# Last layer of a decoder kernel: expert outputs scattered with an add into four DRAM accumulators, in place of eight rows a token

## The chip, the cores and the metric

The kernel runs on one core of one Trainium2 chip. The metric is the time of one execution on the device in microseconds (us); smaller is better. The core has five engines with a queue of instructions each: TensorE (PE; PEld are its weight loads), VectorE (DVE), ScalarE (ACT), GpSimd (POOL) and SyncE (SP). Sixteen DMA engines move data between DRAM and the on-chip memories. Engines wait for one another and for transfers by semaphores.

## The reference

The program is a stack of four layers, each a cross attention and a feed-forward stage with a residual, on x of 8 x 128 tokens of 256 values. Only the last stage, a mixture of 64 experts of which each token takes 8, and each expert at most 128 tokens, bears on the change:

```python
x_rep = jnp.repeat(x, K, axis=0)                                  # K = 8
xe = jnp.zeros((E, C, H), x.dtype).at[flat_e, pos].set(x_rep, mode='drop')   # E = 64, C = 128
gu = jnp.einsum('ech,ehf->ecf', xe, gate_up_proj)
g, u = jnp.split(gu, 2, axis=-1)
h = jax.nn.silu(g) * u
ye = jnp.einsum('eci,eih->ech', h, down_proj)
valid = pos < C
y_flat = jnp.where(valid[:, None], ye[flat_e, jnp.minimum(pos, C - 1)], 0.0)
y = jnp.sum(y_flat.reshape(-1, K, H) * topw.reshape(-1, K)[..., None], axis=1)
...
x = x + _L3_ffn_ref(_layernorm(x, axis=-1), ...)
```

So a token's result is the sum of up to eight expert rows, each times its weight, and x.

## The kernel before

The whole program is written by hand, engine by engine; each stage is a block in which every engine has its own list of instructions in a fixed order, and blocks end in a barrier. Nothing plans the order: what stands in the code is what each queue holds. The last stage is the function `moe_l3`. It has four parts.

**Routing** (PE, DVE, ACT). PE makes the router's logits. DVE finds each token's eight experts (L2334 to L2340, `mask`). From the mask two things are made side by side: PE counts each token's place in its expert's list (`pos`, L2241, 36 small matmuls), and DVE makes a key for every token and expert. The key holds the number of the DRAM row into which this expert's result for this token will go: 8 x token + rank, and the rank comes from a running count over the mask (L2344, L2345, L2347). L2349 then needs both. After a transpose, eight rounds of maximum and replace (L2358, L2361) list each expert's 128 largest keys, and L2364 to L2367 turn these into `slot` (the row for the scatter) and `idx` (the token, slot divided by eight, for the gather). Slots that hold no token point at rows behind the tokens' rows.

**The expert loop.** For each of 64 experts POOL issues an indirect DMA that gathers 128 token rows of x (L2208), PE transposes them and multiplies by the gate and up weights (L2269), ACT and DVE make h, PE transposes h (L2277) and multiplies by the down weights (L2284), ACT scales the rows by the routing weights into one of four buffers `ye` (L2326), and POOL issues an indirect DMA that scatters the 128 rows of 1 KB to DRAM (`rows`, L2213). POOL issues eight gathers first and then, for each scatter, two gathers until 16 are ahead, then one; the last 16 scatters have no gathers between them. Before ACT overwrites a buffer of `ye` it waits until the scatter of four experts ago has landed:

```python
                    if e >= NY:
                        act.wait_ge(put[e % NY], 16 * (e // NY))
```

SP meanwhile loads the experts' weights, 16 loads of 1280 KB, six loads ahead of their use (L2183).

**The sum.** When all scatters have landed, SP reads the rows back in eight loads of 1024 KB, one for each 128 tokens (L2187; each token's eight rows are 8 KB in one piece). DVE adds eight rows to four, to two, to one (L2397) and adds x (L2398), and SP stores the 128 tokens (L2190).

**Zeroing.** A token whose expert was full has no row, so `rows` is set to zero beforehand: eight writes of 1024 KB that SP issues in the attention of layer 1 (L837), some 1100 us earlier. POOL waits for them before the first scatter.

Of the kernel before, what the change touches and what calls it, by code (L numbers as in the profile page):

```python
# [9 lines left out]
I32 = mybir.dt.int32  # L10
U8 = mybir.dt.uint8
U32 = mybir.dt.uint32
ALU = mybir.AluOpType
# [3 lines left out]
P = 128  # L17
D = 256
KD = D // P
B = 8  # L20
T = B * P
# [763 lines left out]
def attention_l1(pg):  # L785
# [5 lines left out]
    const, masks, qm_in, cb_in, vz_in, scores, maxed, nm_turned, augmented, shifted, exped, pv, recip, scaled, added = (  # L791
        pg.sem(f"l1x_{m}") for m in sems)
    with ExitStack() as st:
# [39 lines left out]

        @block.sync
        def _(sp):
            for i in range(8):
                sp.dma_start(pg.l3_rows[T * i:T * (i + 1), :].rearrange("(p r) d -> p r d", p=P),  # L837
                             pg.zero_row[:].unsqueeze(1).to_broadcast([P, T // P, D])).then_inc(pg.rows_zeroed, 16)

# [1278 lines left out]
def moe_l3(pg, pre, xw, rows):  # L2118

    nc, E, K, CAP, F = pg.nc, 64, 8, 128, 96  # L2120
    GROUP, LOADS, AHEAD, FIRST, NY = 4, 6, 16, 8, 4
# [6 lines left out]
    s = {m: pg.sem(f"l3m_{m}") for m in names}  # L2128
    w_in = [pg.sem(f"l3m_w_in{i}") for i in range(LOADS)]
    gathered = [pg.sem(f"l3m_gathered{i}") for i in range(AHEAD)]  # L2130
    put = [pg.sem(f"l3m_put{i}") for i in range(NY)]
    back = [pg.sem(f"l3m_back{i}") for i in range(B)]
    with ExitStack() as st:
        def sb(m, shape, dt=F32):
            return st.enter_context(nc.sbuf_tensor(f"l3m_{m}", shape, dt))
        def wide_of(at, n):
            return pg.l2_wx[:].rearrange("p k n -> p (k n)")[:, at:at + n].rearrange("p (b e) -> p b e", b=B)
# [2 lines left out]
        cw = wide_of(512, B * E)  # L2140
        left = wide_of(1024, B * E)
        mask = sb("mask", [P, B, E], BF16)
        tmp = wide_of(2048, B * E)
        best = sb("best", [P, B, 8])
        top = sb("top", [P, B, 8])
        small = sb("small", [P, 3, B])
# [2 lines left out]
        token = sb("token", [P, B])  # L2149
        row = sb("row", [P, E])  # L2150
        key = wide_of(2560, 2 * B * E)
        spent = pg.l2_w3[:].rearrange("p a k n -> p (a k n)").bitcast(F32)
# [1 line left out]
        lst = sb("lst", [P, CAP // 2])  # L2154
        spare = sb("spare", [P, E])
        idxf = sb("idxf", [P, E])
        count = pg.l2_wx[:].rearrange("p k n -> p (k n)")[:, 3584:3584 + B * E]
        slot = sb("slot", [P, E], I32)
        idx = sb("idx", [P, E], I32)
        zero = sb("zero", [P, ROW])  # L2160
        w = sb("w", [P, LOADS, GROUP, W])
# [2 lines left out]
        h = sb("h", [P, 2, F])  # L2164
        hT = sb("hT", [F, 2, P])
        ye = pg.ctxt[:, 0:NY, :]
        fin = spent[:, 0:B * K * D].rearrange("p (b k d) -> p b k d", b=B, k=K)
        xg = spent[:, 0:AHEAD * ROW].rearrange("p (a n) -> p a n", n=ROW)
        ps = [st.enter_context(nc.psum_tensor(f"l3m_ps{i}", [P, HALF], F32)) for i in range(8)]
        x_ps, gu_ps, h_ps, y_ps = ps[0:2], ps[2:4], ps[4:6], ps[6:8]  # L2170
# [7 lines left out]
        @block.sync  # L2178
        def _(sp):
            for g in range(E // GROUP):  # L2180
                if g >= LOADS:
                    sp.wait_ge(s["y_done"], GROUP * (g - LOADS + 1))
                sp.dma_start(w[:, g % LOADS], pg.dram["l3_moe"][g].rearrange("p (e n) -> p e n", e=GROUP)).then_inc(w_in[g % LOADS], 16)  # L2183
            for i in range(NY):
                sp.wait_ge(put[i], 16 * (E // NY))
            for t in range(B):
                sp.dma_start(fin[:, t], rows[P * K * t:P * K * (t + 1), :].rearrange("(p k) d -> p k d", k=K)).then_inc(back[t], 16)  # L2187
            for t in range(B):
                sp.wait_ge(s["summed"], t + 1)
                sp.dma_start(pg.out[t], fin[:, t, 0, :]).then_inc(s["stored"], 16)  # L2190
            sp.wait_ge(s["stored"], 16 * B)

        @block.gpsimd
        def _(pool):
            g = nc.gpsimd
            g.memset(ones[:], 1.0).then_inc(s["ones_in"], 1)
            g.memset(zero[:], 0.0).then_inc(s["zero_in"], 1)
            pool.wait_ge(s["ones_in"], 1)
            g.affine_select(out=before[:], in_=ones[:], compare_op=ALU.is_gt, fill=0.0, base=0,
                            pattern=[[1, P]], channel_multiplier=-1).then_inc(s["const"], 1)  # L2200
            g.iota(token[:], [[8 - P * K, B]], K * T + 1, -K, allow_small_or_imprecise_dtypes=True).then_inc(s["const"], 1)
            g.iota(row[:], [[0, E // NY], [P, NY]], 0, 1, allow_small_or_imprecise_dtypes=True).then_inc(s["const"], 1)

            def gather(e):
                if e >= AHEAD:
                    pool.wait_ge(s["x_turned"], e - AHEAD + 1)
                    pool.wait_ge(s["y_kept"], e - AHEAD + 1)
                g.indirect_dma_start(out=xg[:, e % AHEAD, :], out_offset=None, in_=xw,  # L2208
                                     in_offset=bass.IndirectOffsetOnAxis(ap=idx[:, e:e + 1], axis=0)).then_inc(gathered[e % AHEAD], 16)

            def scatter(e):
                pool.wait_ge(s["y_kept"], e + 1)
                g.indirect_dma_start(out=rows, out_offset=bass.IndirectOffsetOnAxis(ap=slot[:, e:e + 1], axis=0),  # L2213
                                     in_=ye[:, e % NY, :], in_offset=None).then_inc(put[e % NY], 16)

            pool.wait_ge(s["exped"], B)
            pool.wait_ge(s["top_inverse"], 1)
            g.tensor_tensor(cw[:], ex[:], small[:, 2, :].unsqueeze(2).to_broadcast([P, B, E]), ALU.mult).then_inc(s["weighed"], 1)
            pool.wait_ge(s["indexed"], 1)
            pool.wait_ge(s["table_in"], 48)  # L2220
            for e in range(FIRST):
                gather(e)
            pool.wait_ge(pg.rows_zeroed, 16 * 8)
            for e in range(E):
                scatter(e)
                for n in range(min(FIRST + 2 * e, e + AHEAD), min(FIRST + 2 * e + 2, e + AHEAD + 1)):
                    if n < E:
                        gather(n)

        @block.tensor  # L2230
        def _(pe):
# [2 lines left out]
                for k in range(KD):  # L2234
                    last = nc.tensor.matmul(lg[:, t, :], pg.xnT[:, k, t * P:(t + 1) * P], rw[:, k, :], start=(k == 0), stop=(k == KD - 1))  # L2235
            last.then_inc(s["logits"], 1)
            pe.wait_ge(s["const"], 3)
            pe.wait_ge(s["masked"], 1)
            for t in range(B):
                for u in range(t + 1):  # L2240
# [8 lines left out]
            for g in range(2):  # L2249
                rows = slice(64 * g, 64 * g + 64)  # L2250
# [78 lines left out]
        def _(dve):  # L2329
            v, ch = nc.vector, Chain(dve, s["steps"])  # L2330
            wide = [P, B, E]
# [5 lines left out]
            for n in range(B):  # L2337
# [1 line left out]
            ch.wait()  # L2339
            v.tensor_scalar(mask[:], left[:], GONE, None, ALU.is_le).then_inc(s["masked"], 1)  # L2340
            dve.wait_ge(s["masked"], 1)
            dve.wait_ge(s["const"], 3)
            flat = mask[:].rearrange("p b e -> p (b e)")
            ch.link(v.tensor_tensor_scan(count[:], flat, flat, 0.0, ALU.add, ALU.max))  # L2344
            ch.link(v.scalar_tensor_tensor(out=tmp[:], in0=count[:].rearrange("p (b e) -> p b e", b=B), scalar=-1.0,  # L2345
                                           in1=token[:].unsqueeze(2).to_broadcast(wide), op0=ALU.mult, op1=ALU.add))
            ch.link(v.tensor_tensor(key[:, :, 0:E], tmp[:], mask[:], ALU.mult))  # L2347
            dve.wait_ge(s["ranked"], 1)
            v.scalar_tensor_tensor(out=key[:, :, E:2 * E], in0=pos, scalar=float(CAP // 2), in1=key[:, :, 0:E], op0=ALU.is_ge, op1=ALU.mult)\  # L2349
                .then_inc(s["keyed"], 1)  # L2350
# [13 lines left out]
            ch.link(v.scalar_tensor_tensor(out=spare[:], in0=list_ps[:, 0:E], scalar=0.0, in1=row[:], op0=ALU.is_equal, op1=ALU.mult))  # L2364
            ch.link(v.scalar_tensor_tensor(out=idxf[:], in0=list_ps[:, 0:E], scalar=-1.0, in1=spare[:], op0=ALU.mult, op1=ALU.add))
            ch.link(v.tensor_scalar(slot[:], idxf[:], float(K * T), None, ALU.add))
            v.tensor_scalar(idx[:], slot[:], 3, None, ALU.logical_shift_right).then_inc(s["indexed"], 1)  # L2367

            def keep_x(e):
                dve.wait_ge(s["x_turned"], e + 1)  # L2370
# [22 lines left out]
                    make_h(i - 1)  # L2393
            for t in range(B):
                dve.wait_ge(back[t], 16)
                for n in (4, 2, 1):
                    ch.link(v.tensor_tensor(fin[:, t, 0:n], fin[:, t, 0:n], fin[:, t, n:2 * n], ALU.add))  # L2397
                v.tensor_tensor(fin[:, t, 0], fin[:, t, 0], pg.x[:, t, :], ALU.add).then_inc(s["summed"], 1)  # L2398

# [4 lines left out]
def program(nc, dram, out):  # L2404
    with ExitStack() as ctx:
# [37 lines left out]
        def sparse_l3():  # L2443
            xw = nc.dram_tensor("l3_xw", (T + P, D + 64), F32, kind="Internal").ap()
            with ExitStack() as early:
                pre = Preload(pg, early, "l3r", [("w", [P, KD, 64], dram["l3_router"])])
                norm(pg, "l3n", pg.x, pre.load, moments=pg.moments)
                moe_l3(pg, pre, xw, pg.l3_rows)
# [109 lines left out]
```

## Time and profile before

| | us |
|---|---|
| median of 3 runs | 1818.53 (1818.27 to 1819.35) |
| the profiled execution, its own time | 1817.0 |
| its span, first to last instruction | 1815.3 |
| last stage: routing, 1584.2 to 1619.9 | 35.7 |
| expert loop while gathers are issued, 1619.9 to 1763.4 | 143.5 |
| last 16 scatters, 1763.4 to 1786.0 | 22.6 |
| reading back, sum and store, 1786.0 to 1815.3 | 29.3 |

The profile gives, for one execution, when each instruction ran and what ended the idle time before it. A group of rows is named by line, engine and operation, then what is written and what is read. A DMA's row on an engine is the time in which the engine issues it; its landing is told apart.

### The profile page before, as it was taken

To read this page: it belongs to the slowest core of one execution; us is meant where nothing else is said; L and a number is where in the kernel's file an instruction comes from. 1 tells how busy PE (TensorE), PEld (TensorE's weight loads), DVE (VectorE), ACT (ScalarE), POOL (GpSimd) and SP (SyncE) were. 2 spreads that over 40 slices of the span, in tenths; PEclk is the share of its full clock that TensorE was granted. 3 is DMA by queue.
4 is the path that set the end of the run, shared out by engine and by line. 5 is a ranking of instruction groups with operands and counts; after the bars stand their busy time and mean duration, and the time that the engine had idled before them with its cause. 6 is when DMAs were issued, how large, how long until landed. Compare 5 with 4: busy or idle time off the path is not lost. (4 is left out here: it accounts for less than half of the span.)

```text
span 1815.3 us, 25122 instructions
## 1 busy us (share of the span) xinstructions
PE 1519.1 (84%) x8563; PEld 971.4 (54%) x8600; DVE 1083.3 (60%) x2317; ACT 805.5 (44%) x1879; POOL 801.4 (44%) x975
## 2 busy tenths in 40 slices
PE   7566669999797799998899999999799989836772
PEld 5222235556465356556367777776455565525661
DVE  7999972222665644354778888888722255572336
ACT  3988873111333211111788888888521111412221
POOL 3366641000200289792277787777310000027772
PEclk9666659999698899999999999999899988958896
DMA  2599981110503111310600000000111100056656
GB/s 79 86 182 176 174 150 55 35 44 18 186 2 124 64 55 59 125 50 19 209 1 13 13 13 13 13 13 1 44 30 42 37 25 1 25 219 233 233 172 243
DMA packets 177808, 148.52 MB, mean 82 GB/s; under 512 B 142305, under 2 KB 155233, under 8 KB 173970
## 3 DMA queue, kind: packets, MB, share of 16 engines
q1 hardware_dynamic: 167618, 119.08, 24.3%
q0 software_dynamic: 7696, 26.22, 4.1%
q10 hardware_dynamic: 2368, 1.61, 0.3%
q8 instruction: 70, 1.15, 0.3%
q14 instruction: 56, 0.46, 0.1%
HBM read 89.62 MB, written 23.70 MB: 62 GB/s over the span
## 5 line engine op out<-in xcount | busy, mean ns | idle before, releaser
L1983 POOL CAST l0m_pi<-l0m_pf 128x1024 bf16<-128x1024 int16 x128 | 133.2, 1040 | 88.2 <-ACT l0m_pf L2050 86.4
L421 PE MATMUL l1e_gu<-x_normT,l1e_w 128*128 128x512 f32 x384 | 171.5, 601 | 0.0
L2050 ACT ACTIVATE l0m_pf<-l0m_s,l0m_bias,l0x_sq 128x1024 int16<-128x1024 f32 x128 | 153.9, 1204 | 20.9 <-DVE l0m_bias L2083 14.7
L2079 DVE TENSOR_REDUCE l0m_mx<-l0m_s 128x1 f32<-128x1024 f32 x128 | 155.6, 1216 | 4.4 <-PE l0m_s L1992 4.1
L1558 PE MATMUL l2x_pr<-l_w,l2x_xq 128*128 128x512 bf16 x539 | 133.5, 382 | 8.5 <-ACT credits L42 5.7
L1992 PE MATMUL l0m_s<-l0x_kT,l0x_qT 64*128 64x512 bf16 x256 | 68.0, 552 | 68.5 <-ACT l0m_pf L2050 66.9
L421 PE MATMUL l0e_gu<-x_normT,l0e_w 128*128 128x512 f32 x272 | 121.5, 601 | 0.0
L421 PEld LDWEIGHTS l1e_gu<-x_normT,l1e_w 128*128 128x128 f32 x384 | 74.2, 194 | 84.1 <-issue 83.0
L421 PE MATMUL l2e_gu<-x_normT,l2e_w 128*128 128x512 f32 x256 | 115.0, 604 | 0.0
L1688 DVE BATCH_NORM_STATS2 l2x_bn<-l2x_raw 128x6 f32<-128x128 f32 x384 | 83.3, 280 | 51.7 <-ACT l2x_raw L1627 51.5
L473 ACT ACTIVATE l1e_sil<-l1e_gu 128x512 f32<-128x512 f32 x48 | 28.6, 596 | 178.6 <-PE l1e_gu L421 178.6
L1520 POOL TENSOR_TENSOR l2x_cq<-ctx_tok,l2x_step 128x512 bf16<-128x512 f32 x64 | 74.8, 1169 | 53.5 <-DVE ctx_tok L1316 53.5
L497 DVE TENSOR_TENSOR l1e_h<-l1e_sil,l1e_gu 128x512 f32<-128x512 f32 x40 | 27.5, 688 | 114.4 <-ACT l1e_sil L473 114.4
L1632 ACT ACTIVATE x_norm<-l2x_s,l2x_mx 128x128 f32<-128x128 f32 x256 | 90.1, 369 | 11.7 <-DVE l2x_mx L1693 11.7
L1558 PEld LDWEIGHTS l2x_pr<-l_w,l2x_xq 128*128 128x128 bf16 x576 | 56.5, 98 | 57.1 <-ACT credits L42 6.1
L428 PE MATMUL l1e_y<-l1e_w,l1e_h 128*128 128x256 f32 x384 | 86.2, 379 | 0.0
L497 DVE TENSOR_TENSOR l0e_h<-l0e_sil,l0e_gu 128x512 f32<-128x512 f32 x28 | 19.3, 688 | 111.3 <-ACT l0e_sil L473 111.3
L421 PEld LDWEIGHTS l0e_gu<-x_normT,l0e_w 128*128 128x128 f32 x272 | 52.4, 194 | 59.9 <-issue 59.2
L1536 POOL TENSOR_TENSOR l2x_rs<-l2x_rs,l2x_half 128x8 f32<-128x8 f32 x48 | 81.2, 1693 | 3.8
L428 PEld LDWEIGHTS l1e_y<-l1e_w,l1e_h 128*128 128x128 f32 x384 | 73.1, 190 | 18.3 <-issue 9.6
L1540 POOL TENSOR_TENSOR x_norm<-x_norm,l2x_rsm 128x512 f32<-128x512 f32 x64 | 73.3, 1145 | 21.4 <-DVE l2x_rsm L1702 20.6
L2208 POOL DMA_INDIRECT l_w<-l_xw,l3m_idx x64 | 61.9, 968 | 41.5 <-DVE l3m_idx L2367 22.3
(438 smaller groups left out, 3597.1 us busy)
## 6 DMA issues: line engine op xcount, KB each, us to landing
l3m_w<-in_l_moe SPq DMA_DIRECT2D x16, 1280.0 KB, 6.9
l1e_w<-in_l_ffn SPq DMA_DIRECT2D x24, 384.0 KB, 3.1
l_rows<-zero_row SPq DMA_DIRECT2D x8, 1024.0 KB, 10.9
l_w<-l_rows SPq DMA_DIRECT2D x8, 1024.0 KB, 11.3
l0e_w<-in_l_ffn SPq DMA_DIRECT2D x17, 384.0 KB, 3.1
l2e_w<-in_l_ffn SPq DMA_DIRECT2D x16, 384.0 KB, 3.0
ctx_tok<-l_route SPq DMA_DIRECT2D x8, 512.0 KB
l2q_wps<-in_l_wp SPq DMA_DIRECT2D x16, 256.0 KB, 3.5
```

The costliest lines, as they stand in the source:

```text
L421: last = nc.tensor.matmul(gu[half][:, m, :], w[:, c % SW, (2 * k + m) * P:(2 * k + m + 1) * P], pg.xnT[:, k, cols(n)], start=(k == 0), sto ...
L428: last = nc.tensor.matmul(y[:, t, :], h[:, c % SH, t * P:(t + 1) * P], w[:, c % SW, WG:CHUNK], start=(c == 0 and t % 2 == 0), stop=False, ...
L1520: nc.gpsimd.tensor_tensor(cq[:, a], wide[:, a % 2], step[:, a % 2], ALU.subtract).then_inc(s["quanted"], 1)
L1536: g.tensor_tensor(rs[:, 1, two, :], var, half[:, 0], ALU.pow).then_inc(s["rstd"], 1)
L1540: nc.gpsimd.tensor_tensor(p[:, a % 2], p[:, a % 2], rsm[:, a % 2].unsqueeze(2).to_broadcast([P, U, P]), ALU.mult).then_inc(s["p_normed"], 1)
L1558: last = nc.tensor.matmul(flat(pr[n % 2][:]), src[:, k, tokens], pg.l2_w3[:, part, k, at:at + W], start=(k == 0 and part == 0), stop=(k == ...
L1632: last = nc.scalar.activation(p[:, a % 2, j, :], s_ps[a % 2][:, j, :], ACT.Exp, bias=mx[:, a % 2, j:j + 1], accum_out=sm[:, a % 2, j:j + 1])
L1688: last = nc.vector.bn_stats(bn[:, t, j, :], raw[:, t, j, :])
L1983: nc.gpsimd.tensor_copy(pi[:, n % 8, :], pf[:, n % 4, :]).then_inc(s["rounded"], 1)
L1992: last = nc.tensor.matmul(s_ps[n % 3][:, g * HALF:(g + 1) * HALF], qT[g * R:(g + 1) * R, h, b * P:(b + 1) * P], kT[g * R:(g + 1) * R, h, : ...
L2050: nc.scalar.activation(pf[:, n % 4, :], s_ps[n % 3][:], ACT.Exp, scale=sq[:, h, b:b + 1], bias=bias[:, n % 4:n % 4 + 1], accum_out=sm[:, b ...
L2079: nc.vector.tensor_reduce(mx[:, n % 4:n % 4 + 1], s_ps[n % 3][:], AX, ALU.max).then_inc(s["maxed"], 1)
```

## The change

An expert's scatter now adds its rows to what stands in DRAM. There are four accumulators of 1024 + 128 rows; expert e adds into accumulator e mod 4, at the row of the token (`dest` = `idx` + e mod 4 times 1152). Two experts that share an accumulator may hold the same token, so the scatter of expert e waits until that of expert e - 4 has landed. At the end a token's four rows, 1152 rows apart, are read and summed, where it was eight rows in one piece. The key needs the token alone, so the running count and one more DVE step go; one integer add for `dest` and one constant on POOL (`sums`) come. Five blocks of 1024 rows are set to zero, where it was eight.

```diff
-            for i in range(8):
+            for i in range(5):
                 sp.dma_start(pg.l3_rows[T * i:T * (i + 1), :].rearrange("(p r) d -> p r d", p=P),
...
-                sp.dma_start(fin[:, t], rows[P * K * t:P * K * (t + 1), :].rearrange("(p k) d -> p k d", k=K)).then_inc(back[t], 16)
+                sp.dma_start(fin[:, t], rows[0:NY * (T + P), :].rearrange("(a r) d -> r a d", a=NY)[P * t:P * (t + 1)]).then_inc(back[t], 16)
...
+            g.iota(sums[:], [[0, E // NY], [T + P, NY]], 0, 0).then_inc(s["const"], 1)
...
             def scatter(e):
                 pool.wait_ge(s["y_kept"], e + 1)
-                g.indirect_dma_start(out=rows, out_offset=bass.IndirectOffsetOnAxis(ap=slot[:, e:e + 1], axis=0),
-                                     in_=ye[:, e % NY, :], in_offset=None).then_inc(put[e % NY], 16)
+                if e >= NY:
+                    pool.wait_ge(put[e % NY], 16 * (e // NY))
+                g.indirect_dma_start(out=rows, out_offset=bass.IndirectOffsetOnAxis(ap=dest[:, e:e + 1], axis=0),
+                                     in_=ye[:, e % NY, :], in_offset=None, compute_op=ALU.add).then_inc(put[e % NY], 16)
...
-            dve.wait_ge(s["const"], 3)
-            flat = mask[:].rearrange("p b e -> p (b e)")
-            ch.link(v.tensor_tensor_scan(count[:], flat, flat, 0.0, ALU.add, ALU.max))
-            ch.link(v.scalar_tensor_tensor(out=tmp[:], in0=count[:].rearrange("p (b e) -> p b e", b=B), scalar=-1.0,
-                                           in1=token[:].unsqueeze(2).to_broadcast(wide), op0=ALU.mult, op1=ALU.add))
-            ch.link(v.tensor_tensor(key[:, :, 0:E], tmp[:], mask[:], ALU.mult))
+            dve.wait_ge(s["const"], 4)
+            ch.link(v.tensor_tensor(key[:, :, 0:E], token[:].unsqueeze(2).to_broadcast(wide), mask[:], ALU.mult))
...
-            v.tensor_scalar(idx[:], slot[:], 3, None, ALU.logical_shift_right).then_inc(s["indexed"], 1)
+            ch.link(v.tensor_scalar(idx[:], slot[:], 3, None, ALU.logical_shift_right))
+            v.tensor_tensor(dest[:], idx[:], sums[:], ALU.add).then_inc(s["indexed"], 1)
...
-                for n in (4, 2, 1):
+                for n in (2, 1):
```

On POOL, at the fourth to sixth scatter of the loop, the queue held this before. The names of semaphores are those of first use: `l0e_routed` stands for `y_kept`, `l0r_const_in` for `x_turned`.

```order
L2208 DMA l2_w3<-l3_xw,l3m_idx 128x320 x2
L2213 DMA l3_rows<-ctx_tok,l3m_slot 8704x256 [waits l0e_routed]
L2208 DMA l2_w3<-l3_xw,l3m_idx 128x320 x2
L2213 DMA l3_rows<-ctx_tok,l3m_slot 8704x256 [waits l0e_routed]
L2208 DMA l2_w3<-l3_xw,l3m_idx 128x320 [waits l0e_routed,l0r_const_in] x2
L2213 DMA l3_rows<-ctx_tok,l3m_slot 8704x256 [waits l0e_routed]
```

And now, with `l1x_pv` and `l1x_recip` standing for the landing of the scatters into the first and the second buffer (`put`):

```order
L2209 DMA l2_w3<-l3_xw,l3m_idx 128x320 x2
L2216 DMA l3_rows<-ctx_tok,l3m_dest 8704x256 [waits l0e_routed]
L2209 DMA l2_w3<-l3_xw,l3m_idx 128x320 x2
L2216 DMA l3_rows<-ctx_tok,l3m_dest 8704x256 [waits l1x_pv,l0e_routed]
L2209 DMA l2_w3<-l3_xw,l3m_idx 128x320 [waits l0e_routed,l0r_const_in] x2
L2216 DMA l3_rows<-ctx_tok,l3m_dest 8704x256 [waits l1x_recip,l0e_routed]
```

The order and the number of POOL's DMAs stay; from the fifth scatter on each has one wait more.

On DVE, from the mask of the eight experts to the reciprocal behind the keys, before:

```order
L2340 TENSOR_SCALAR l3m_mask<-l_wx 128x512
L2344 SCALAR_TENSOR_TENSOR l_wx<-l3m_mask 128x512
L2345 SCALAR_TENSOR_TENSOR l_wx<-l_wx,l3m_token 128x512
L2347 TENSOR_TENSOR l_wx<-l_wx,l3m_mask 128x8x64
L2349 SCALAR_TENSOR_TENSOR l_wx<-l3m_ps,l_wx 128x8x64
L2352 RECIPROCAL l3m_small<-l3m_small 128x8
```

And now, from one step ahead of the mask:

```order
L2341 MATCH_REPLACE l_wx<-l3m_best,l3m_ps 128x64 x8
L2343 TENSOR_SCALAR l3m_mask<-l_wx 128x512
L2346 TENSOR_TENSOR l_wx<-l3m_token,l3m_mask 128x8x64
L2348 SCALAR_TENSOR_TENSOR l_wx<-l3m_ps,l_wx 128x8x64
L2351 RECIPROCAL l3m_small<-l3m_small 128x8
```

Two steps are gone between the mask and the step (L2349, now L2348) that also reads PE's counts.

## Rows read from the trace of the kernel before

**Rows 1.** Window of the loop: us; PE, PEld, DVE, ACT, POOL busy; clock; DMA; GB/s.
```profile
1619.90:1763.40 143.50, 102.01 (x487) 82.57 (x487) 47.22 (x161) 35.62 (x105) 109.38 (x112) 0.87 0.61 208
```
**Rows 2.** Timeline of POOL, the loop: start, us, instruction, [idle before <-releaser].
```profile
1619.87 1.11 POOL L2208 DMA_INDIRECT l_w<-l_xw,l3m_idx  x1 [22.32 <-DVE l3m_idx L2367]
...
1630.07 1.02 POOL L2213 DMA_INDIRECT l_rows<-ctx_tok,l3m_slot  x1 [0.30 <-issue]
...
1762.14 0.97 POOL L2208 DMA_INDIRECT l_w<-l_xw,l3m_idx  x1 [0.30 <-issue]
1763.42 0.99 POOL L2213 DMA_INDIRECT l_rows<-ctx_tok,l3m_slot  x1 [0.30 <-issue]
1764.71 0.99 POOL L2213 DMA_INDIRECT l_rows<-ctx_tok,l3m_slot  x1 [0.30 <-issue]
...
1783.59 0.97 POOL L2213 DMA_INDIRECT l_rows<-ctx_tok,l3m_slot  x1 [0.62 <-ACT ctx_tok L2326]
```
**Rows 3.** One line's view of the scatters (L2213): issue, idle, waiters, landing.
```profile
L2213 POOL DMA_INDIRECT l_rows<-ctx_tok,l3m_slot x64: 967/988/1017, 1630.1 to 1783.6; - x64
  ACT ctx_tok L2326: 65.0, 27
DMA to landing us min/median/max: 2.4/2.4/7.2
```
**Rows 4.** The same view of the gathers (L2208): landing.
```profile
DMA to landing us min/median/max: 2.8/2.9/6.9
```
**Rows 5.** Line views of POOL's two other kinds of DMA: issue ns min/median/max.
```profile
L1373 POOL DMA_DIRECT2D l_vc<-l2q_vc x16: 540/540/668, 868.9 to 893.6; - x16
L93 POOL DMA_DIRECT2D l_raw<-in_l_w x1: 950/950/950, 733.0 to 733.0; - x1
```
**Rows 6.** Timeline of DVE and PE, the routing.
```profile
1592.55 1.23 DVE L2344 TENSOR_TENSOR_SCAN l_wx<-l3m_mask 128x512 f32<-128x512 bf16 x1
...
1594.50 0.24 PE L2241 MATMUL l3m_ps<-l3m_mask,l3m_before 128*128 128x64 bf16 x1
1594.54 0.69 DVE L2347 TENSOR_TENSOR l_wx<-l_wx,l3m_mask 128x512 f32<-128x512 f32 x1
1595.26 0.69 DVE L2349 SCALAR_TENSOR_TENSOR l_wx<-l3m_ps,l_wx 128x512 f32<-128x512 f32 x1
...
1618.89 0.23 DVE L2365 SCALAR_TENSOR_TENSOR l3m_idxf<-l3m_ps,l3m_spare 128x64 f32<-128x64 f32 x1
```
**Rows 7.** Timeline of the end.
```profile
1786.05 4.14 SPq L2187 DMA_DIRECT2D l_w<-l_rows  x8
1790.82 2.41 DVE L2397 TENSOR_TENSOR l_w<-l_w 128x1024 f32<-128x1024 f32 x3 [8.77 <-DMA l_w<-l_rows]
...
1793.61 2.40 DVE L2397 TENSOR_TENSOR l_w<-l_w 128x1024 f32<-128x1024 f32 x3
...
1796.39 2.40 DVE L2397 TENSOR_TENSOR l_w<-l_w 128x1024 f32<-128x1024 f32 x3
...
1812.72 0.43 DVE L2398 TENSOR_TENSOR l_w<-l_w,x_res 128x256 f32<-128x256 f32 x1
```
**Rows 8.** Chain that ended last, one 128-token tile of it: start, us, what.
```profile
1810.37 1.15 DVE l_w L2397
```
**Rows 9.** Line views of loads: landing of L146 (two of 512 KB), then L2187.
```profile
L146 SPq DMA_DIRECT2D x_res<-in_x x2: 457/474/492, 0.8 to 1.3; - x2
...
DMA to landing us min/median/max: 4.1/4.5/5.0
...
DMA to landing us min/median/max: 4.8/11.3/19.8
```
**Rows 10.** Line view of ACT's scaling step (L2326).
```profile
L2326 ACT ACTIVATE ctx_tok<-l3m_ps,l_w x64: 473/473/477, 1628.6 to 1782.8; 128x256 f32<-128x256 f32 x64
```
**Rows 11.** Timeline of SP around the zeroing.
```profile
478.89 6.02 SPq L837 DMA_DIRECT2D l_rows<-zero_row  x2
573.71 0.33 SPq L2435 DMA_DIRECT2D l1r_w<-in_l_router  x1
```

More of the change, by code:

```diff
@@ L2142, in moe_l3 @@
         mask = sb("mask", [P, B, E], BF16)
-        tmp = wide_of(2048, B * E)
         best = sb("best", [P, B, 8])
@@ L2156, in moe_l3 @@
         idxf = sb("idxf", [P, E])
-        count = pg.l2_wx[:].rearrange("p k n -> p (k n)")[:, 3584:3584 + B * E]
         slot = sb("slot", [P, E], I32)
+        sums = sb("sums", [P, E], I32)
+        dest = sb("dest", [P, E], I32)
         idx = sb("idx", [P, E], I32)
@@ L2166, in moe_l3 @@
         ye = pg.ctxt[:, 0:NY, :]
-        fin = spent[:, 0:B * K * D].rearrange("p (b k d) -> p b k d", b=B, k=K)
+        fin = spent[:, 0:B * NY * D].rearrange("p (b a d) -> p b a d", b=B, a=NY)
         xg = spent[:, 0:AHEAD * ROW].rearrange("p (a n) -> p a n", n=ROW)
@@ L2200, in _ @@
                             pattern=[[1, P]], channel_multiplier=-1).then_inc(s["const"], 1)
-            g.iota(token[:], [[8 - P * K, B]], K * T + 1, -K, allow_small_or_imprecise_dtypes=True).then_inc(s["const"], 1)
-            g.iota(row[:], [[0, E // NY], [P, NY]], 0, 1, allow_small_or_imprecise_dtypes=True).then_inc(s["const"], 1)
+            g.iota(token[:], [[-P * K, B]], K * T, -K, allow_small_or_imprecise_dtypes=True).then_inc(s["const"], 1)
+            g.iota(row[:], [[0, E]], 0, K, allow_small_or_imprecise_dtypes=True).then_inc(s["const"], 1)
+            g.iota(sums[:], [[0, E // NY], [T + P, NY]], 0, 0).then_inc(s["const"], 1)
             def gather(e):
@@ L2222, in _ @@
                 gather(e)
-            pool.wait_ge(pg.rows_zeroed, 16 * 8)
+            pool.wait_ge(pg.rows_zeroed, 16 * 5)
             for e in range(E):
@@ L2236, in _ @@
             last.then_inc(s["logits"], 1)
-            pe.wait_ge(s["const"], 3)
+            pe.wait_ge(s["const"], 4)
             pe.wait_ge(s["masked"], 1)
```

## Prediction

> **What bounds the kernel now.** I read the windows of the last stage first, then POOL's timeline through the expert loop, then the view of the scatter's line, and the end last. The rest of the program is not touched, except for the zeroing.
>
> The expert loop lasts 143.5 us while gathers are issued; PE is busy for 102.0 of them and POOL for 109.4 [rows 1]. That looks like a stage with slack everywhere, and it is not. In POOL's timeline one indirect DMA follows the other: a scatter's row is 0.99 us long, a gather's 0.97, and before nearly each stands 0.30 us whose releaser is "issue", which means that POOL waited for nothing [rows 2]. The step from one start to the next is 1.28 to 1.29 us. 64 gathers and 48 scatters at 1.28 make 143.4 us, the stretch itself. So POOL sets the pace, one expert each 2.57 us, and whatever lengthens a scatter's issue lengthens the loop one for one.
>
> The waits of ACT tell something else: 65.0 us, 27 times, until a scatter has landed [rows 3]. That is the ring of four `ye` buffers. It costs nothing as it stands, since ACT, and PE behind it, only run ahead of POOL until the ring is full: POOL comes back to a buffer after 4 x 2.57 = 10.3 us, and the longest landing is 7.2 [rows 3].
>
> The last 16 scatters have no gathers between them. POOL could take one each 1.28 us, but near the end it waits for ACT (the last of [rows 2]); from 1763.42 to 1783.59 it is 20.2 us for 15 steps. Then SP starts the loads at 1786.05, DVE gets the first tile at 1790.82, and from there DVE works without a gap, 2.78 us a tile (1793.61 to 1796.39), until 1813.15; the last store ends the span at 1815.3 [rows 7].
>
> **The change part by part.**
>
> The sum at the end. The widest of DVE's three additions goes: 1.15 us [rows 8] and the 0.02 between links. A tile then takes 2.78 - 1.17 = 1.61 us, and eight save 9.4. The loads must keep up: 512 KB a tile, now in runs of 1 KB. Two loads of this size and run length landed after 4.1 and 5.0 us and were issued 0.5 us apart, so the second took 1.4 us more [rows 9]; seven more tiles at 1.4 are ready before DVE wants them at 1.61. The margin is thin; at 1.8 us a tile the gain would be 8. The first load lands after 4.1 instead of 4.8 us [rows 9]: -0.65. Together -10.0, between -8 and -11.
>
> Routing. The running count (1.23) and the step behind it go, but not off the path: L2349 also needs PE's counts, and the last of these ends at 1594.74, when L2349 starts at 1595.26 today [rows 6]. So 0.45 us of the 1.9 come back. The integer add for `dest` costs a small DVE step, 0.23 [rows 6], and POOL's gathers wait for it. Together -0.2. The extra constant on POOL lies in its idle 22.3 us ahead of the first gather [rows 2].
>
> Zeroing. Three writes of 1 MB fewer; SP's next DMA comes 89 us after the last of them is issued [rows 11], and nobody waits for them before. Nothing.
>
> The added wait. POOL now waits before scatter e for the landing of scatter e - 4. Behind it in the queue stand the gathers and, through them, all of PE. But ACT waits for the same landing before it writes the buffer, and POOL already waits for ACT: when POOL gets there the wait is fulfilled. As an instruction it is also free: the gathers late in the loop carry two waits, the scatters one, and all have 0.30 us before them [rows 2]. Nothing, as long as ACT's wait stands.
>
> The scatter itself is the open price, twice.
>
> *Its issue on POOL.* An add in DRAM has to read two rows and write one, where a copy reads one and writes one, and POOL writes the lists of what is to be read and written. No row shows such a DMA. Two direct DMAs of POOL bound it: 128 runs of 2 KB (L1373) are issued in 0.54 us, 256 runs of 12 KB (L93, 128 partitions by two) in 0.95 [rows 5]. So 128 runs more, read and write, cost 0.41 us; the read alone would be 0.2 if the two are written one after the other. Below that stands zero (a fixed part that hides it), above a second issue of the whole, 0.99 [rows 2]. I take 0.3 us, the middle of 0.2 and 0.41, since the pair of rows is the only one in which the count differs.
>
> The Trainium skill ("DMA: Bandwidth & Descriptors", section on the anatomy of one DMA on the GpSimd path) calls descriptor generation "small, variable" and says one can emit many before the incremental cost shows; by that the term would be 0 and the time that of the first rival. The two rows above do not look like it: the issue nearly doubles with the runs. Its page "Collectives: The Full Stack" (the section on the bandwidth ceiling) says of the adding DMA that it emits two read descriptors per chunk; no run here shows that yet.
>
> With 0.3: 48 scatters among gathers give 14.4 us. The last 16 then step at 1.28 + 0.3 = 1.58 us, 15 of them 23.7 against 20.2 today, +3.5 (less than 15 x 0.3, because POOL's waits there are filled).
>
> *Its landing.* A plain scatter lands after 2.4 us, a gather, which reads DRAM, after 2.9 [rows 3, 4]. An add that reads DRAM and writes it lies between 2.4 and the two in a row, 5.3. I take 3.0, near the gather, and the 0.3 of issue: +0.9 on the last landing, on the path. In the loop it is covered by the ring: 10.3 us of return against at most 7.2.
>
> **The sum**, against the profiled execution's 1817.0 us: loop +14.4, last scatters +3.5, last landing +0.9, routing -0.2, end -10.0. That is +8.6, 1825.6. The median of the runs shown lies 1.5 above the profiled one; the forecast for the median is 1818.5 + 8.6 = **1827**. With 0.2 of issue: 9.6 + 2.0 + 0.8 - 10.2 = +2.2, 1821. With 0.41: 19.7 + 5.1 + 1.0 - 10.2 = +15.6, 1834. The two sides meet near 0.17 us a scatter.
>
> **The rivals.**
>
> *The issue does not grow* (faster). If the fixed part of an indirect DMA, 0.99 against the 0.54 of the direct one of 128 runs, hides the second read, the loop stays, and only landings count: 0.6 for the last ring turn and 0.6 for the last landing. 1.2 - 10.2 = -9.0, **1809.5**. For it: the indirect DMA has 0.45 us that don't come from the runs. Against it: the row to be added to is itself looked up by index.
>
> *The ring decides* (slower). If reading, adding and writing wait for one another in the loaded stretch, a landing could grow to the longest scatter and the longest gather in a row, 7.2 + 6.9 = 14.1 us [rows 3, 4]. The turn of the ring is then 14.1 + 0.47 for ACT [rows 10] + 0.3 to POOL's start = 14.9 us, 3.7 per expert instead of 2.57, and at the 27 experts where ACT waits for a landing today that is 31 us: 1818.5 + 31 - 9 = **1840**. It decides from a landing of 9.5 us on (10.3 less 0.8). For it: DMA engines are 61% busy in the loop [rows 1] and each scatter gets half as much again to move. Against it: the typical landing is 2.4, a quarter of that.
>
> *The add is issued like a second DMA* (much slower): 0.99 a scatter. 47.5 + 15 x 2.27 - 20.2 = 61.4, and 1.6 - 10.2: +53, **1871**.
>
> **How the numbers follow.** About 0.2% (3.6 us) is what a measurement of this kernel can tell from no change. Forecast (0.2 to 0.41): 0.43, of which 0.10 ends within 0.2%. No growth (up to 0.1): 0.32, nearly all faster, 0.02 within. The ring: 0.13. The second DMA: 0.12. So faster 0.30, same 0.12, slower 0.58. The range has to reach the first rival and the ring; it leaves out the second DMA: 1806 (1809.5 with the end at its better bound and no longer landings) to 1845 (the ring with a little of the issue's growth).
>
> **What would show it.** POOL's rows of the scatter: 1.3 us where they were 0.99, with 0.30 before them, says that the forecast is right; 0.99 the first rival; idle time before them that ACT or a landing ends, with ACT's wait well over 65 us, the ring. The distance of the expert loop's first to last scatter, 153.5 us now, should be 171 to 172. At the end DVE's tiles should step at 1.61 us; steps that a load ends would show that the loads do not keep up. L2348 should be released by PE. I am wrong if issue grows by less than 0.17 or more than 0.5 us, or if the landing passes 9.5.

## Result and profile after

| | before | after |
|---|---|---|
| median, us | 1818.94 (1818.27 to 1820.73, 4 runs) | 1845.36 (1845.12 to 1846.79, 4 runs) |
| span of the profiled execution | 1815.3 | 1843.7 |

The ratio is 1.0145, 95% interval 1.0131 to 1.0159: the change makes the kernel slower, by 26.4 us. The forecast was 1827 (+8.6) in a range of 1806 to 1845. The direction was right, the size was not, and the time lies just outside the range.

Where the time went is read from POOL's timeline through the expert loop of the changed kernel (start, us, instruction, idle time before it and what ended it). L2216 is the adding scatter, L2209 the gather.

```profile
1619.93 1.11 POOL L2209 DMA_INDIRECT l_w<-l_xw,l3m_idx  x1 [22.86 <-DVE l3m_dest L2367]
...
1630.12 1.65 POOL L2216 DMA_INDIRECT l_rows<-ctx_tok,l3m_dest  x1 [0.30 <-issue]
...
1738.03 0.99 POOL L2209 DMA_INDIRECT l_w<-l_xw,l3m_idx  x1 [0.30 <-issue]
1739.33 1.59 POOL L2216 DMA_INDIRECT l_rows<-ctx_tok,l3m_dest  x1 [0.30 <-issue]
...
1821.42 1.55 POOL L2216 DMA_INDIRECT l_rows<-ctx_tok,l3m_dest  x1 [0.30 <-issue]
```

The idle time before a scatter is 0.30 us as in [rows 2], but the scatter's own row is 1.59 us where it was 0.99. From the first scatter to the last it is 191.3 us now and was 153.5. The view of the scatter's line gives the same for all 64, and the landing (issue in ns, then who waited, then the landing in us):

```profile
L2216 POOL DMA_INDIRECT l_rows<-ctx_tok,l3m_dest x64: 1553/1588/1647, 1630.1 to 1821.4; - x64
  ACT ctx_tok L2329: 112.0, 46
DMA to landing us min/median/max: 3.6/3.8/7.9
```

Against [rows 3] the median issue is 0.60 us longer and the landing, counted from the start of the issue, 1.4 longer; 0.6 of the 1.4 is the issue itself. ACT waits 112 us in place of 65 for landings, and yet POOL goes on without a gap: the ring is fuller, and still not the bound.

The end, which answers to [rows 7] (SP's loads of the four rows, then DVE's tiles):

```profile
1825.28 7.43 SPq L2187 DMA_DIRECT2D l_w<-l_rows  x8
```
```profile
1829.02 1.15 DVE L2397 TENSOR_TENSOR l_w<-l_w 128x512 f32<-128x512 f32 x2 [13.29 <-DMA l_w<-l_rows]
...
1832.36 1.15 DVE L2397 TENSOR_TENSOR l_w<-l_w 128x512 f32<-128x512 f32 x2 [0.20 <-DMA l_w<-l_rows]
...
1833.89 1.14 DVE L2397 TENSOR_TENSOR l_w<-l_w 128x512 f32<-128x512 f32 x2
...
1835.41 1.14 DVE L2397 TENSOR_TENSOR l_w<-l_w 128x512 f32<-128x512 f32 x2
```

A tile steps at 1.52 us (1833.89 to 1835.41) where it was 2.78, and one tile waits 0.20 us for its load. From SP's first load to the end of the span it is 18.4 us and was 29.3.

The routing, which answers to [rows 6]:

```profile
1592.76 0.69 DVE L2346 TENSOR_TENSOR l_wx<-l3m_token,l3m_mask 128x512 f32<-128x512 f32 x1
1595.07 0.69 DVE L2348 SCALAR_TENSOR_TENSOR l_wx<-l3m_ps,l_wx 128x512 f32<-128x512 f32 x1 [1.61 <-PE l3m_ps L2244]
...
1619.42 0.23 DVE L2367 CUSTOM_DVE_ANT_0 l3m_dest<-l3m_idx,l3m_sums 128x128 uint16<-128x128 uint16 x1
```

DVE now waits 1.61 us for PE's counts: of the two steps removed nearly all turned into a wait, and `dest` took 0.23.

The balance between the two profiled executions: first to last scatter +37.8, last landing +1.4, routing -0.2, end -10.8 (29.25 to 18.42), the start of the stage +0.2. Together +28.4, the difference of the spans. The profiled execution of the kernel before lies 1.9 us below its median, which is why the medians differ by 26.4.

### The profile page after: what moved, and what is told of

It is laid out like the page before. It is cut to its first block and busy times, and to the rows that moved or that the text cites. A ratio compares the mean times of both kernels' runs of the same rounds, so it can differ in the third digit from the quotient of the medians.

```text
span 1843.7 us, 25171 instructions
## 1 busy us (share of the span) xinstructions
PE 1531.2 (83%) x8563; PEld 979.7 (53%) x8600; DVE 1071.7 (58%) x2308; ACT 805.5 (44%) x1879; POOL 841.9 (46%) x976
## 3 DMA queue, kind: packets, MB, share of 16 engines
q10 hardware_dynamic: 2368, 1.61, 0.3%
q8 instruction: 70, 1.15, 0.3%
HBM read 85.43 MB, written 20.55 MB: 57 GB/s over the span
## 5 line engine op out<-in xcount | busy, mean ns | idle before, releaser
L2050 ACT ACTIVATE l0m_pf<-l0m_s,l0m_bias,l0x_sq 128x1024 int16<-128x1024 f32 x128 | 154.0, 1206 | 20.3 <-DVE l0m_bias L2083 14.0
L2216 POOL DMA_INDIRECT l_rows<-ctx_tok,l3m_dest x64 | 101.5, 1586 | 19.5 <-issue 18.0
L2379 DVE TENSOR_TENSOR l3m_h<-l3m_sil,l3m_ps 128x96 f32<-128x96 f32 x64 | 16.3, 254 | 117.5 <-ACT l3m_sil L2323 117.5
```

The lines of the kernel that those rows point to most:

```text
L2050: nc.scalar.activation(pf[:, n % 4, :], s_ps[n % 3][:], ACT.Exp, scale=sq[:, h, b:b + 1], bias=bias[:, n % 4:n % 4 + 1], accum_out=sm[:, b ...
```

## Experiments

Theory after the comparison: the adding DMA costs POOL 0.6 us more to issue, POOL is the bound of the loop, so 64 x 0.6 lands in the time. Rivals: the added wait, the new row addresses, the ring; and, for the 0.6 itself, whether it goes by rows, by bytes, by the look-up of a second index, or is a fixed price.

**The change without its add.** One edit to the changed kernel; rows of one token overwrite one another, so that the sums leave out most of the expert rows:

```diff
-                                     in_=ye[:, e % NY, :], in_offset=None, compute_op=ALU.add).then_inc(put[e % NY], 16)
+                                     in_=ye[:, e % NY, :], in_offset=None).then_inc(put[e % NY], 16)
```

> The changed kernel with the scatter as a plain copy into the same accumulators (rows of the same token overwrite one another, so the sums at the end leave out most expert rows); all else stays: the added wait, dest, the four-row read-back. Theory (the add itself lengthens POOL's issue from 0.985 to 1.588 us and the landing from 2.4 to 3.8): scatter's issue back at 0.99, first to last scatter back from 191.3 to 153.5 us, so 1845.4 - 37.8 - 1.4 = about 1806. Rival (the wait, the new row addresses or the ring lengthen the scatter): issue stays over 1.2 us and the time over 1815.

Measured: 1808.5 us (1807.95 to 1810.21), against the kernel before 0.9943 (0.9926 to 0.9960). The scatter's line and landing:

```profile
L2216 POOL DMA_INDIRECT l_rows<-ctx_tok,l3m_dest x64: 965/988/1010, 1632.7 to 1786.2; - x64
DMA to landing us min/median/max: 2.4/2.4/6.8
```

Issue, landing and the 153.5 us from first to last scatter are those of the kernel before. So the added wait, the new addresses and the 1 KB runs at the end cost nothing that shows; all but the add gains 10 us, and the add costs 37 (1845.4 - 1808.5).

**The add alone.** The reverse edit on the kernel before: its scatter, into eight rows a token that are each written once, adds to the zeros.

```diff
-                                     in_=ye[:, e % NY, :], in_offset=None).then_inc(put[e % NY], 16)
+                                     in_=ye[:, e % NY, :], in_offset=None, compute_op=ALU.add).then_inc(put[e % NY], 16)
```

> The kernel before with one edit: its scatter adds to the zeroed eight-row layout, where every row is written once. Theory (price of the add, wherever it goes): issue 1.59 us, first to last scatter 191 us, landing 3.8, so 1818.9 + 37.8 + 1.4 = 1858. Rival (the price comes from adding twice to the same row, or from the wait for the scatter four before): issue about 1.0 and 1819 to 1825.

Measured: 1858.46 us (1856.39 to 1866.2), ratio 1.0230 (1.0206 to 1.0254).

```profile
L2213 POOL DMA_INDIRECT l_rows<-ctx_tok,l3m_slot x64: 1553/1587/1643, 1630.2 to 1821.5; - x64
DMA to landing us min/median/max: 3.7/3.8/7.4
```

The forecast of 1858 is met. The price belongs to the DMA that adds, whether a row has been added to before or not.

**Without POOL's added wait.** ACT's wait for the same landing stays.

```diff
-                if e >= NY:
-                    pool.wait_ge(put[e % NY], 16 * (e // NY))
```

> The changed kernel without POOL's wait for the scatter of four experts ago (ACT's wait for the same landing stays and orders the two). Theory (wait is fulfilled when POOL comes to it): 1845.4 within 0.1%, 0.30 us between POOL's DMAs as now. Rival (the wait instruction costs 0.05 us in POOL's queue): 60 x 0.05 = 3 us less, 1842.

Measured: 1847.57 us (1845.86 to 1852.47), ratio 1.0161 (1.0142 to 1.0180), which overlaps that of the changed kernel.

```profile
L2214 POOL DMA_INDIRECT l_rows<-ctx_tok,l3m_dest x64: 1554/1588/1648, 1632.5 to 1824.0; - x64
```

191.5 us from first to last scatter, against 191.3 with the wait. The wait is free, as the prediction had it.

**What the 0.6 us goes by.** The changed kernel with scatters of four sizes, one line each, once adding and once copying (the four accumulators lie twice as far apart, eight blocks are zeroed; rows and halves that a size doesn't send are left out of the sums):

```diff
+                if e % NY == 0:
+                    g.indirect_dma_start(... ap=dest[0:P, e:e + 1] ... in_=ye[0:P, e % NY, 0:D] ...)
+                elif e % NY == 1:
+                    g.indirect_dma_start(... ap=dest[0:P // 2, e:e + 1] ... in_=ye[0:P // 2, e % NY, 0:D] ...)
+                elif e % NY == 2:
+                    g.indirect_dma_start(... ap=dest[0:P // 4, e:e + 1] ... in_=ye[0:P // 4, e % NY, 0:D] ...)
+                else:
+                    g.indirect_dma_start(... ap=dest[0:P, e:e + 1] ... in_=ye[0:P, e % NY, 0:D // 2] ...)
```

> The changed kernel with adding scatters of four sizes, by expert modulo four: 128 rows of 1 KB, 64 rows of 1 KB, 32 rows of 1 KB, 128 rows of 512 B (the other halves are left out; accumulators twice as far apart, eight blocks zeroed). To be read beside the same with copies. Theory A (an entry more per row): issue 1.59, then lower by about 0.30 and 0.45 beyond what a copy saves, and 1.59 for the 512 B rows. Theory B (a fixed price of the adding path): the add is 0.6 over the copy at every number of rows. Theory C (bytes): the 512 B rows save as much as the 64 rows.

> The four sizes of the adding run, as plain copies into the same places (the sums leave out what is overwritten and what is not sent). The adds took 1.59, 1.46, 1.36 and 1.60 us of issue for 128, 64, 32 rows of 1 KB and 128 of 512 B. Theory (a mostly fixed price of the adding path): copies 0.99, about 0.90, 0.85 and 0.99, the add 0.5 above them even at 32 rows. Rival (price per row): the distance shrinks to a quarter, 0.15, at 32 rows, so a copy of 32 rows would take 1.2, more than one of 128.

The lines of the adding kernel (128, 64, 32 rows, then 128 half rows; ns min/median/max):

```profile
L2217 POOL DMA_INDIRECT l_rows<-ctx_tok,l3m_dest x16: 1559/1593/1644, 1632.4 to 1813.1; - x16
L2219 POOL DMA_INDIRECT l_rows<-ctx_tok,l3m_dest x16: 1422/1461/1498, 1636.9 to 1815.0; - x16
L2221 POOL DMA_INDIRECT l_rows<-ctx_tok,l3m_dest x16: 1337/1364/1398, 1641.3 to 1816.7; - x16
L2223 POOL DMA_INDIRECT l_rows<-ctx_tok,l3m_dest x16: 1561/1596/1633, 1645.5 to 1818.4; - x16
```

And of the copying one:

```profile
L2217 POOL DMA_INDIRECT l_rows<-ctx_tok,l3m_dest x16: 969/988/1010, 1632.4 to 1778.8; - x16
L2219 POOL DMA_INDIRECT l_rows<-ctx_tok,l3m_dest x16: 899/912/924, 1636.2 to 1780.4; - x16
L2221 POOL DMA_INDIRECT l_rows<-ctx_tok,l3m_dest x16: 864/874/896, 1640.0 to 1782.0; - x16
L2223 POOL DMA_INDIRECT l_rows<-ctx_tok,l3m_dest x16: 975/987/1001, 1643.7 to 1783.6; - x16
```

| | add | copy | the add's price |
|---|---|---|---|
| 128 rows of 1 KB | 1.593 | 0.988 | 0.605 |
| 64 rows of 1 KB | 1.461 | 0.912 | 0.549 |
| 32 rows of 1 KB | 1.364 | 0.874 | 0.490 |
| 128 rows of 512 B | 1.596 | 0.987 | 0.609 |

From 128 rows to 32 the copy loses 0.114 us, 1.2 ns a row, and the price of the add another 0.115. Bytes do not count. So 0.49 us of the 0.605 is still there at a quarter of the rows: theory B, the fixed price, with a small share of A. Fewer than 32 rows were not run; carried on to none, the slope over all three sizes or over the last two leaves 0.43 to 0.45 us, an estimate. (One run each, 1841.6 and 1805.9 us as a whole; with sizes mixed, only their rows matter here.)

**Is it the second look-up by index?** POOL's scatters as direct DMAs to fixed rows (nothing is sorted to tokens):

```diff
+                if e % NY == 0:
+                    g.dma_start(rows[0:P, :], ye[:, e % NY, :], accum_op=ALU.add).then_inc(put[e % NY], 16)
+                elif e % NY == 1:
+                    g.dma_start(rows[P:2 * P, :], ye[:, e % NY, :]).then_inc(put[e % NY], 16)
+                elif e % NY == 2:
+                    g.dma_start(rows[2 * P:2 * P + P // 2, :], ye[0:P // 2, e % NY, :], accum_op=ALU.add).then_inc(put[e % NY], 16)
+                else:
+                    g.dma_start(rows[3 * P:3 * P + P // 2, :], ye[0:P // 2, e % NY, :]).then_inc(put[e % NY], 16)
```

> The changed kernel with POOL's scatters as direct DMAs without an index (to fixed rows, so nothing is sorted to tokens): by expert modulo four an add of 128 rows of 1 KB, a copy of 128, an add of 64, a copy of 64. Theory P (the adding path has its own price): direct copy about 0.54 us of issue, direct add about 1.14. Theory L (the price is the second look-up by index): direct add at most 0.75.

In the order of the diff:

```profile
L2217 POOL DMA_DIRECT2D l_rows<-ctx_tok x16: 879/1008/1049, 1631.7 to 1761.7; - x16
L2219 POOL DMA_DIRECT2D l_rows<-ctx_tok x16: 570/642/980, 1635.3 to 1763.4; - x16
L2221 POOL DMA_DIRECT2D l_rows<-ctx_tok x16: 849/964/1317, 1638.5 to 1764.9; - x16
L2223 POOL DMA_DIRECT2D l_rows<-ctx_tok x16: 559/639/1294, 1642.1 to 1767.5; - x16
```

Neither theory as put: by the medians the direct add is 0.37 us over the direct copy at 128 rows and 0.33 at 64. Most of these rows stand right behind a gather; where POOL had been idle before, the rows are shorter:

```profile
1755.22 0.89 POOL L2217 DMA_DIRECT2D l_rows<-ctx_tok  x1 [1.09 <-ACT ctx_tok L2335]
1756.84 0.57 POOL L2219 DMA_DIRECT2D l_rows<-ctx_tok  x1 [0.73 <-ACT ctx_tok L2335]
```

That is 0.32 us for the add of 128 rows, and 0.28 for that of 64 (0.85 against 0.57 just after). So 0.3 to 0.4 of the 0.60 is there without an index, most of it fixed; the other 0.2 to 0.3 shows only in the indirect DMA. The fixed rows also lie in one piece in DRAM, so the index and the scattered places went together, and that a second look-up makes the difference is not shown. (One run, 1789.5 us.)

**POOL relieved.** Gathers for the first 16 experts alone, in the changed kernel and in the one before; the other experts compute on those rows again.

```diff
-                    if n < E:
+                    if n < AHEAD:
...
-                pe.wait_ge(gathered[e % AHEAD], 16 * (e // AHEAD) + 16)
+                pe.wait_ge(gathered[e % AHEAD], 16)
```

> The changed kernel with gathers for the first 16 experts alone (the others compute on those rows again), so that POOL has an adding scatter an expert and nothing else for most of the loop: 1.89 us an expert, PE's own step is 1.62. Theory (POOL is the bound of the loop also with the add; the ring is not): about 8 x 1.3 fewer... first to last scatter 63 x 1.89 + 8 x 1.29 = 129 us. Rival (ring and landing become the bound once POOL is relieved: 7.9 us landing and 0.8 on a turn of 7.6): over 135 us, with POOL idle before scatters because of ACT or a landing.

> The kernel before with gathers for the first 16 experts alone: POOL's scatter is 1.28 us an expert, less than PE's 1.62. Theory (POOL bounds the loop of the kernel before): first to last scatter falls from 153.5 to the PE's step, 63 x 1.62 = 102 us or a little more where a landing of up to 7.2 holds a turn of 6.5. Rival (PE or the transfers already bound it): over 135 us.

The scatter's lines of the two, the changed kernel first; the lines under them are what ended POOL's idle time before a scatter (us, times). The last two lines tell the same of ACT, ahead of its scaling step, in the second of the two kernels:

```profile
L2216 POOL DMA_INDIRECT l_rows<-ctx_tok,l3m_dest x64: 1552/1553/1642, 1630.2 to 1767.9; - x64
  issue: 16.5, 54
  DMA l_rows<-ctx_tok,l3m_dest: 7.3, 5
  ACT ctx_tok L2329: 5.7, 5
...
DMA to landing us min/median/max: 3.7/4.0/10.1
```
```profile
L2213 POOL DMA_INDIRECT l_rows<-ctx_tok,l3m_slot x64: 969/969/1016, 1632.9 to 1745.9; - x64
  ACT ctx_tok L2326: 39.3, 55
  issue: 2.7, 9
```
```profile
  PE l3m_ps L2284: 22.1, 59
  DMA l_rows<-ctx_tok,l3m_slot: 11.7, 4
```

In the kernel before, 153.5 us became 113.0, and POOL now waits for ACT before 55 of 64 scatters: POOL was the bound of that loop. The 11 us over the 102 of PE's step are about what ACT waited for four landings (11.7). The gathers' transfers are gone here too; the direct DMAs above shorten POOL's rows with the gathers in place, and there first to last scatter took 135.8 us. In the changed kernel 191.3 became 137.7, where 129 was expected. Before ten scatters POOL's idle time, 13.0 us in all, ended with a landing or with ACT; seven of these waits are longer than the usual 0.30 us, by 10.0 us together. So here the rival has its place: once a turn of the ring is 7.4 us (4 x 1.86), landings of up to 10.1 us hold it. In the changed kernel a turn is 12.7 us while gathers are issued, against landings of at most 7.9; in its last 16 scatters it is 7.4 too, but no landing there takes more than 5.3, and POOL has no wait over 0.31. (One run each, 1791.8 and 1779.4 us.)

**A version that beats both.** The end is worth 10 us as long as POOL's scatter stays a copy. So the bytes were halved instead of the rows: ACT rounds the scaled expert rows to bfloat16, and PE sums a token's eight rows in f32. (The zeroing, the type of `rows` and the stores follow suit and are left out here.)

```diff
-        ye = pg.ctxt[:, 0:NY, :]
+        ye = pg.ctxt[:].rearrange("p b d -> p (b d)").bitcast(BF16)[:, 0:NY * D].rearrange("p (b d) -> p b d", b=NY)
...
+            for t in range(B):
+                pe.wait_ge(back[t], 16)
+                for k in range(K):
+                    last = nc.tensor.matmul(ps[t][:, 0:D], pg.identb[:], fin[:, t, k, :], start=(k == 0), stop=(k == K - 1))
+                last.then_inc(s["y_done"], 1)
...
-                for n in (4, 2, 1):
-                    ch.link(v.tensor_tensor(fin[:, t, 0:n], fin[:, t, 0:n], fin[:, t, n:2 * n], ALU.add))
-                v.tensor_tensor(fin[:, t, 0], fin[:, t, 0], pg.x[:, t, :], ALU.add).then_inc(s["summed"], 1)
+                v.tensor_tensor(pg.x[:, t, :], ps[t][:, 0:D], pg.x[:, t, :], ALU.add).then_inc(s["summed"], 1)
```

> The kernel before, with the end shortened in another way that leaves POOL's scatter a plain copy: ACT writes the scaled expert rows in bfloat16 (rounded there, a change of precision), so scatters, the zeroing and the eight loads at the end have half the bytes, and PE sums a token's eight rows by eight matmuls with the identity into f32, DVE adds x. Theory (POOL's issue is the bound of the loop and goes by the number of DMAs, not by their bytes; the end was worth 10 us): scatter's issue 0.99 us, first to last scatter 153.5, end 29.3 to about 20 us, so 1818.9 - 9 = 1810. Rival (the end is bound by PE's 64 matmuls or by what SP issues): end 25 us or more, 1815 and up.

Measured: 1809.1 us (1806.45 to 1811.01, 5 runs), ratio 0.9940 (0.9926 to 0.9953). The scatter's line, then SP's loads at the end:

```profile
L2213 POOL DMA_INDIRECT l_rows<-ctx_tok,l3m_slot x64: 968/990/1017, 1633.8 to 1787.8; - x64
```
```profile
1790.11 3.71 SPq L2187 DMA_DIRECT2D l_w<-l_rows  x8
```

The issue is 0.99 us for half the bytes, the loop 154.0 us, and the end 17.8 us (1790.11 to the end of the span at 1807.9). The version is faster than both kernels, at the price of rows rounded to bfloat16.

## Why the prediction was right and wrong

**POOL as the bound of the loop: right.** The whole lengthening of the scatter landed in the time, and with gathers taken away the loop of the kernel before fell to 113.0 us, near PE's step, with POOL waiting.

**The issue of the adding scatter: the step that failed.** The term was 0.3 us, with 0.2 to 0.41 as its range and 0.5 as its sign of being wrong; it is 0.60. With 0.60 the prediction's own sum gives 48 x 0.60 + 15 x 1.88 - 20.2 = 36.8 for the loop, where 37.8 was measured, so the rest of the working holds. The 1.0 left is about what the 56 gathers behind the first scatter took more: their median row went from 0.97 to 0.99 us, which no term had. What was wrong is the reading of [rows 5]. Two direct DMAs that differ in runs (128 and 256), in run length and in direction were taken to differ by their runs. The size experiment shows that a row of an indirect copy costs 1.2 ns, so that 128 more would be worth 0.15 us, and direct copies of 64 and 128 rows are issued in 0.64 us alike: 0.41 was not the price of 128 runs. What makes the longer of the two so long was not tested. And an add was priced as more entries of a list, when 0.49 of its 0.605 us remains with a quarter of the rows. The row to look at with suspicion was [rows 2] beside [rows 5]: an indirect DMA takes 0.99 us where a direct one of as many runs takes 0.54, so POOL has large costs that don't go by the count. The prediction saw them, and drew on them only for the rival that the issue does not grow. What the fixed price of an add consists of stays open.

The rule of the Trainium skill that was weighed there ("DMA: Bandwidth & Descriptors", the anatomy of one DMA on the GpSimd path: many descriptors can be emitted before the incremental cost shows) was nearer to the truth on the count than the prediction: 96 rows more of a copy cost 0.11 us. It did not bear the conclusion drawn from it, the first rival at 1809.5, since the add's price is not one of count. What the prediction takes from the Trainium skill's "Collectives: The Full Stack" (the section on the bandwidth ceiling: two read descriptors per chunk) is said there of the reduce step of a collective; for POOL's adding DMA no count of these runs shows a second read.

**Its landing: right in kind, short.** +0.9 was forecast, +1.4 measured: 0.6 of issue in place of 0.3, and 0.8 for the add in place of 0.6. In the loop the ring covered it, as forecast.

**The end: right.** -10.0 forecast, -10.8 measured: tiles step at 1.52 us, not 1.61, and the first load landed after 3.7 us, not 4.1. The 1.15 us of [rows 8] are the widest addition without the part that lies over the end of the tile before; its whole row is 1.22 (mean 1219 ns), and the addition that is now the first of a tile overlaps in its place. The loads kept up but for 0.2 us.

**Routing, zeroing, the added wait: right.** Routing gave 0.2 us; L2348 is released by PE, as written. The wait on POOL costs nothing, with the cover named: ACT's wait for the same landing.

**The rivals.** That the issue does not grow: excluded by the profile. The second DMA (0.99): too much, and farther from 0.60 than the forecast's 0.3. The ring: not in this kernel; it becomes a bound only with POOL relieved. The range ended at 1845, the ring's case with a little of the issue's growth, because the forecast's bound for the issue, 0.41, was treated as firm: from 0.41 to 0.99 no case stood, and the truth, 0.60, fell there. That the time lies only just outside is owed to the ring's case, which did not happen. (For the lower end the prediction's own terms give 1807, not 1806; nothing hangs on it.)

## What to carry to other kernels

Before moving an addition into a DMA, ask who issues it and whether that engine has time. Here GpSimd was busy without a gap, though its busy share read 76%, because the 0.30 us ahead of each indirect DMA are part of its price; 0.6 us more per DMA cost 38 us where the saved reads gave back 11. And a price for an operation that the trace does not show should be bounded by a measured change of that one thing; two rows that differ in three respects bound nothing.

## What the runs showed of the hardware

- An indirect scatter that adds takes POOL 1.59 us to issue for 128 rows, a copying one 0.99; a direct add 1.01, a direct copy 0.64 (0.89 and 0.57 where POOL had been idle before). Between 32 and 128 rows a row counts 1.2 ns for the indirect copy, about 2.4 for the indirect add; row length between 512 B and 1 KB counts nothing. The indirect add takes 1.55 us in the last 16 scatters as well, where nearly nothing else moves data, so its length does not come from other transfers.
- An adding scatter lands 3.8 us after its issue begins, a copying one 2.4, of 128 rows; these are the medians of all 64 and of the last 16, where nearly nothing else moves data.
- GpSimd's queue in the profile's third part has the same bytes and nearly twice the packets, of before and of after:

```profile
q0 software_dynamic: 7696, 26.22, 4.1%
```
```profile
q0 software_dynamic: 13840, 26.22, 6.6%
```

  6144 packets more over 64 scatters are 96 each: a copy's rows go several to a packet, an added row goes by itself (128 in place of 32). This framing is not the fixed part of POOL's price: the add of 32 rows in the size run goes in 32 packets and 16 small ones, as many as a copy of 128 rows, and takes 1.36 us to issue where that copy takes 0.99. One such add, from 1811.5 to 1813.2 us:

```profile
DMA packets 48, 0.03 MB, mean 19 GB/s; under 512 B 16, under 2 KB 48, under 8 KB 48
```

  Whether the second row to be read makes up the fixed part, the runs do not tell; the page counts 85.43 MB read from DRAM and 20.55 written for the changed kernel with its add and without it.
- An indirect DMA had at least 0.30 us of idle time before it wherever it stood; the direct ones that followed a gather had none:

```profile
1700.70 0.99 POOL L2209 DMA_INDIRECT l_w<-l_xw,l3m_idx  x1 [0.30 <-issue]
1701.69 1.01 POOL L2217 DMA_DIRECT2D l_rows<-ctx_tok  x1
```
